# One TensorE signal per slot, and per pair of slots, in a graph network's two gather stages

## What is computed

```python
x = _layernorm(x + L0(x, edge_attr_64, ...))
x = _layernorm(x + L1(x, edge_attr_64, ...))
# L0:
h = concatenate([x[src], edge_attr], axis=1) @ W1 + b1
msg = silu(batchnorm(h) * g1 + be1)
agg = segment_sum(msg, dst) / maximum(count(dst), 1)
out = silu(batchnorm(concatenate([x, agg], axis=1) @ W2 + b2) * g2 + be2)
# L1:
msg = relu(x[src] + edge_attr)
out = relu(((1 + eps) * x + segment_sum(msg, dst)) @ W.T + b)
```

## Time and profile before

| | us |
|---|---|
| runs | 10119.3, 10121.98, 10125.19; median 10121.98 |
| profiled execution, first to last instruction (span) | 10108.7 |
| POOL busy | 5970.4 (59%) |
| PE busy / PEld busy | 4398.6 (44%) / 2780.5 (28%) |
| DVE / ACT busy | 1864.3 (18%) / 1239.0 (12%) |
| gathers of the first stage (line 371), 3125 | 2968.4 busy, first start 29.5, last 4588.5 |
| gathers of the second stage (line 1194), 3125 | 2971.8 busy, first start 5445.6, last 9967.5 |

### The profile page before, as it was taken

One profiled execution on the slowest core, in us unless ns is written; L12 is line 12 of the kernel. 1 busy time (PEld: TensorE's weight loads), 2 busy tenths in 40 slices (PEclk: granted clock), 3 DMA queues, 4 the chain that ended last, 5 costly groups with the idle time before them and its releaser, 6 DMA issues. The chain is left out here.

```text
span 10108.7 us, 90454 instructions
## 1 busy us (share of the span) xinstructions
PE 4398.6 (44%) x25778; PEld 2780.5 (28%) x25778; DVE 1864.3 (18%) x4868; ACT 1239.0 (12%) x2056; POOL 5970.4 (59%) x6272
## 2 busy tenths in 40 slices
PE   3433443434444444347984333333333334333335
PEld 1222222222222222226872222222222222222222
DVE  2111111111111111116763000000000000000002
ACT  0000000000000000004664000000000000000001
POOL 6666666666666666660003666666666666666662
PEclk7666666666666666668996666666666666666666
DMA  3222222222222222224551121121112212111111
GB/s 79 68 67 66 69 67 66 69 67 67 68 67 68 68 67 67 68 67 132 164 151 50 44 47 45 45 45 45 45 45 45 45 45 46 44 45 45 45 45 33
DMA packets 800217, 638.49 MB, mean 63 GB/s; under 512 B 532451, under 2 KB 618703, under 8 KB 799368
## 3 DMA queue, kind: packets, MB, share of 16 engines
q1 hardware_dynamic: 553308, 326.50, 12.0%
q0 software_dynamic: 200416, 208.55, 10.7%
q10 hardware_dynamic: 46400, 102.52, 3.1%
HBM read 528.15 MB, written 108.90 MB: 63 GB/s over the span
## 5 line engine op out<-in xcount | busy, mean ns | idle before, releaser
L1194 POOL DMA_INDIRECT X<-x_scratch,src_idx x3125 | 2971.8, 951 | 1624.3 <-issue 893.6
L371 POOL DMA_INDIRECT Z<-in_x_dram,src_idx x3125 | 2968.4, 950 | 1611.1 <-issue 895.1
L416 PE MATMUL PS<-ZT,W_sb 128*64 128x320 f32 x2500 | 1198.0, 620 | 2716.5 <-ACT ZT L456 2391.7
L1216 PE MATMUL PS<-hot_c,msg_c 128*64 128x48 f32 x6250 | 658.9, 271 | 2765.6 <-issue 1733.5
L1216 PEld LDWEIGHTS PS<-hot_c,msg_c 128*64 128x64 f32 x6250 | 575.0, 184 | 3163.0 <-issue 2048.4
L416 PEld LDWEIGHTS PS<-ZT,W_sb 128*64 128x64 f32 x2500 | 396.7, 185 | 3153.5 <-issue 2160.2
L522 DVE BATCH_NORM_STATS2 stats<-PS 128x320 f32 (+1 forms) x624 | 279.3, 490 | 3670.2 <-remote 3451.3
L456 ACT ACTIVATE ZT<-PS 128x640 f32<-128x640 f32 x625 | 425.2, 702 | 4150.2 <-remote 3395.5
L1252 DVE TENSOR_TENSOR table<-table,PS 64x48 f32 x625 | 130.2, 208 | 4057.3 <-DMA shares_scratch<-counts 3495.7
L1235 ACT ACTIVATE msg_c<-PS 128x320 f32<-128x320 f32 x625 | 260.0, 436 | 4295.3 <-DMA counts_scratch<-table 2919.9
L1205 PE MATMUL PS<-E,ident 128*128 128x320 f32 x1250 | 689.6, 644 | 11.8 <-DMA E<-in_edge_attr_dram 11.8
(11 more groups left out here) (135 smaller groups left out, 2519.8 us busy)
## 6 DMA issues: line engine op xcount, KB each, us to landing
Z<-in_edge_attr_dram SPq DMA_DIRECT2D x625, 160.0 KB
E<-in_edge_attr_dram SPq DMA_DIRECT2D x625, 160.0 KB
h_scratch<-h_ring ACTq DMA_DIRECT2D x312, 320.0 KB
hT<-h_scratch SPq DMA_DIRECT2D x312, 320.0 KB
Z<-in_x_dram,src_idx POOLq DMA_INDIRECT x3125
X<-x_scratch,src_idx POOLq DMA_INDIRECT x3125
x_nodes<-in_x_dram SPq DMA_DIRECT2D x1, 3125.0 KB
x_ring<-in_x_dram SPq DMA_DIRECT2D x25, 125.0 KB
```

Of the source, the lines that this page charges most:

```text
L371: nc.gpsimd.indirect_dma_start(out=Z[:, r, j, 0:D], out_offset=None, in_=x, in_offset=bass.IndirectOffsetOnAxis(ap=src_idx[:, n:n + 1], ax ...
L416: nc.tensor.matmul(PS[ab * D:(ab + 1) * D, bank + c, 0:HC], W1_sb[:, :], ZT[:, s % 2, c * HC:(c + 1) * HC], start=True, stop=True)
L1194: nc.gpsimd.indirect_dma_start(out=X[:, r, j, :], out_offset=None, in_=x1_dram, in_offset=bass.IndirectOffsetOnAxis(ap=src_idx[:, n:n + 1] ...
L1216: last = nc.tensor.matmul(PS[D:P, 2 + s % S, 0:WIN], msg[:, s % S, j, :], hot[:, s % S, j, :], start=(j == 0), stop=(j == TG - 1))
```

## The change

The first gather stage keeps its work, and its signals `rows_done` and `dense_done` become one, `pe_step`, given once for the first transposes and then at the end of every `dense(s)`; as PE's order is `turn_rows(s + 1)`, `dense(s)`, the value s + 2 tells of both. All who waited for either now wait for it.

The second gather stage works in pairs of slots: one edge load, one relu, one one-hot of two slots, and one signal `pe_step` after the pair's segment sums in place of `sum_put` and `summed` per slot. Edge sums take PSUM banks 0-3, segment sums 4-7. POOL waits at even slots only. The diff, cut (waits of SP, the written-out last slot and some DVE lines are left out):

```diff
-            rows_done = sem("rows_done")
+            pe_step = sem("a_pe_step")
...
-            dense_done = sem("dense_done")
...
-                            pool.wait_ge(rows_done, g + 1 - RING)
+                            pool.wait_ge(pe_step, g + 1 - RING)
...
                             last = nc.tensor.transpose(banks(2 * (s % 2), 2, P, EG)[:, j * P:(j + 1) * P],
                                                        Z[:, r, j, :], ident[:, :])
-                        last.then_inc(rows_done, 1)
+                        return last
...
                                                     hot[:, q % 5, ab, j, :], start=(j == 0), stop=(j == TG - 1))
-                        last.then_inc(dense_done, 1)
+                        last.then_inc(pe_step, 1)
...
-                    turn_rows(0, 0)
+                    turn_rows(0, 0).then_inc(pe_step, 1)
...
-                            act.wait_ge(rows_done, at(k, BODY, s + 1))
-                            wait_at(act, dense_done, k, BODY, s - 1)
+                            act.wait_ge(pe_step, at(k, BODY, s + 1))
...
-                        dve.wait_ge(dense_done, at(k, BODY, 2 * q + 2))
+                        dve.wait_ge(pe_step, at(k, BODY, 2 * q + 3))
...
-            E = sb(here, "E", [P, RING, TG, D])
+            E = sb(here, "E", [P, S, 2, TG, D])
...
-            msg = sb(here, "msg_c", [P, S, TG, D])
-            hot = sb(here, "hot_c", [P, S, TG, WIN])
+            msg = sb(here, "msg_c", [P, 2, 2, TG, D])
+            hot = sb(here, "hot_c", [P, 2, 2, TG, WIN])
...
-                        if g >= RING:
-                            pool.wait_ge(sum_put, g + 1 - RING)
+                        if g >= RING and g % 2 == 0:
+                            pool.wait_ge(pe_step, (g - RING) // 2 + 1)
...
-                    def edge_sum(k, s):
-                        r = s % RING
-                        wait_at(pe, msg_ready, k, BODY, s - 1)
...
+                    def edge_sum(k, q, slots):
+                        wait_at(pe, msg_ready, k, 10, q - 1)
+                        pe.wait_ge(e_loaded[q % S], at(k, 32, 16 * (q // S) + 16))
+                        for a in range(slots):
+                            r = (2 * q + a) % RING
+                            to = PS[:, 2 * (q % 2) + a, 0:HC]
+                            nc.tensor.matmul(to, ident[:, :], E[:, q % S, a, :, :].rearrange("p t c -> p (t c)"),
+                                             start=True, stop=False)
+                            pe.wait_ge(gathered[r], at(k, 32 * TG, 16 * TG * (2 * q // RING) + 16 * TG))
+                            last = nc.tensor.matmul(to, ident[:, :], X[:, r, :, :].rearrange("p t c -> p (t c)"),
+                                                    start=False, stop=True)
+                        return last
+
+                    def segment_sum(k, q, slots):
+                        pe.wait_ge(hot_ready, at(k, 10, q + 1))
+                        pe.wait_ge(msg_ready, at(k, 10, q + 1))
+                        wait_at(pe, added, k, BODY, 2 * q - 2)
+                        for a in range(slots):
+                            for j in range(TG):
+                                last = nc.tensor.matmul(PS[D:P, 4 + 2 * (q % 2) + a, 0:WIN], msg[:, q % 2, a, j, :],
+                                                        hot[:, q % 2, a, j, :], start=(j == 0), stop=(j == TG - 1))
+                        last.then_inc(pe_step, 1)
...
+                        for q in range(slots // 2):
+                            edge_sum(k, q + 1, 1 if slots < BODY and q + 1 == slots // 2 else 2)
+                            segment_sum(k, q, 2)
...
+                    def relu(k, q, slots):
+                        act.wait_ge(pe_step, at(k, 10, q + 1))
+                        act.activation(msg[:, q % 2, 0:slots, :, :].rearrange("p a t c -> p a (t c)"),
+                                       PS[:, 2 * (q % 2):2 * (q % 2) + slots, 0:HC], ACT.Relu).then_inc(msg_ready, 1)
...
+                    def one_hot(k, q, slots):
+                        wait_at(dve, pe_step, k, 10, q)
...
+                    def add(k, s, firsts):
+                        dve.wait_ge(pe_step, at(k, 10, s // 2 + 2))
```

More of the change, by code:

```diff
@@ L1211, in segment_sum @@
-                    def segment_sum(k, s):
-                        pe.wait_ge(hot_ready, at(k, BODY, s + 1))
-                        pe.wait_ge(msg_ready, at(k, BODY, s + 1))
-                        wait_at(pe, added, k, BODY, s + 1 - S)
-                        for j in range(TG):
-                            last = nc.tensor.matmul(PS[D:P, 2 + s % S, 0:WIN], msg[:, s % S, j, :], hot[:, s % S, j, :],
-                                                    start=(j == 0), stop=(j == TG - 1))
-                        last.then_inc(summed, 1)
@@ L1220, in body @@
-                    def body(k, slots):
-                        for s in range(slots):
-                            if not (slots < BODY and s == slots - 1):
-                                edge_sum(k, s + 1)
-                            segment_sum(k, s)
-                    edge_sum(0, 0)
+                    def edge_sum(k, q, slots):
[10 more added lines that the diff above has]
+                        return last
@@ L1227, in _ @@
+                    def body(k, slots):
+                        for q in range(slots // 2):
+                            edge_sum(k, q + 1, 1 if slots < BODY and q + 1 == slots // 2 else 2)
+                            segment_sum(k, q, 2)
+                        if slots < BODY:
+                            segment_sum(k, slots // 2, 1)
+                    edge_sum(0, 0, 2).then_inc(pe_step, 1)
                     all_bodies(pe, body)
@@ L1230, in _ @@
                 def _(act):
+                    def relu(k, q, slots):
+                        act.wait_ge(pe_step, at(k, 10, q + 1))
+                        act.activation(msg[:, q % 2, 0:slots, :, :].rearrange("p a t c -> p a (t c)"),
+                                       PS[:, 2 * (q % 2):2 * (q % 2) + slots, 0:HC], ACT.Relu).then_inc(msg_ready, 1)
                     def body(k, slots):
[L1232 to L1236 removed]
+                        for q in range(slots // 2):
+                            relu(k, q, 2)
+                        if slots < BODY:
+                            relu(k, slots // 2, 1)
                     all_bodies(act, body)
@@ L1249, in add @@
-                    def add(k, s, first):
-                        dve.wait_ge(summed, at(k, BODY, s + 1))
+                            hot[:, q % 2, 0:slots, :, :].rearrange("p a t w -> p (a t) w"),
+                            window[:, :].unsqueeze(1).to_broadcast([P, slots * TG, WIN]),
+                            rel5[:, ds(at(k, BODY, 2 * q), slots), :].rearrange("p a t -> p (a t)").unsqueeze(2)
+                            .to_broadcast([P, slots * TG, WIN]), ALU.is_equal).then_inc(hot_ready, 1)
@@ L1255, in body @@
                     def body(k, slots):
-                        for s in range(slots):
-                            if s % S == 0:
-                                load_windows(dve, at(k, 4, s // S))
-                                firsts = windows_of_turn(dve)
-                            if not (slots < BODY and s == slots - 1):
-                                one_hot(k, s + 1)
-                            add(k, s, firsts[s % S])
-                    one_hot(0, 0)
+                        firsts = {}
@@ new lines, in body @@
+                        for q in range(slots // 2):
+                            for t in range(-(-2 * q // S), (2 * q + 1) // S + 1):
+                                firsts[t] = load_pair_windows(dve, at(k, 4, t), t % 2)
+                            one_hot(k, q + 1, 1 if slots < BODY and q + 1 == slots // 2 else 2)
+                            add(k, 2 * q, firsts)
+                            add(k, 2 * q + 1, firsts)
+                        if slots < BODY:
+                            add(k, 2 * (slots // 2), firsts)
@@ L1265, in _ @@
+                    one_hot(0, 0, 2)
                     all_bodies(dve, body)
```

43 lines of the change are left out of this document (14 added, 29 removed).

## The result

The changed kernel takes 10141.49 us (median of 20 runs, 10130.47 to 10149.35) against 10122.22 (20 runs, 10108.18 to 10133.9): ratio **1.0017, 95% interval 1.001 to 1.0023**. The forecast was 10056, faster; the range, 9520 to 10180, holds the measured time, but it is wide enough for either direction, and the direction was wrong. The profiled spans are 10142.4 and 10108.7 us. The 13 us between span and median that I carried over from before are not there after, where the span is 1.8 us under the time of its own execution: most of the 13 us will have been a quick profiled execution. So the spans show 34 us where the medians show 19, and what a stage differs by from the profile of before may be some 12 us too large.

A forecast was written before the change was run, and what follows sets the result against it. The prediction took POOL's gathers, plus its stops while TensorE's finished signals are held, to bound the kernel. Second stage -124, first stage +50, its end +8: -66 us, from 10121.98 to 10056 us, range 9520 to 10180.

The forecast's parts named there:

- the second stage's term: Second gather stage: one signal per pair gives runs of 16 slots, 0.75 us of stop per slot instead of 0.95, -124 us.
- I take their median, 12.: Second stage: TensorE's signal is held 12 us, the median of six held times from 6.9 to 28.1; hence 15.3 us per pair.
- the low end of my term: Second stage, signal held 28 us: runs of only six slots, 0.92 us of stop per slot, -20 us.
- The stop line: POOL's stops: length follows a straight line, 1.9 us + 0.13 per gather in the run before.
- All a change beside the gathers can win: 1232 us: Both gather stages: POOL's stops of 640 and 592 us are all that can be won, 12% of the span.
- counted as 0: Second stage: VectorE's one-hot for two slots at once runs beside POOL and costs nothing.
- +50 taken: First stage: one signal under way at a time, runs half of three slots (+100 us), half of four (0); +50 us.
- 8 were taken: End of the first stage: TensorE works off ten slots with one more ACT round each, about +8 us.
- Rival 3: Both stages: signals are not what is short, runs and stops stay as they are; 10122 us within 20, chance 0.12.
- one passage in 12.55 us: Second stage, argument against rival 3: two slots need only one signal passage in 12.55 us; rows show 8.3 and 6.9.
- Rival 1: Second stage: signals held under 9.2 us, so POOL never stops; -534 us, 9588 us, chance 0.23.
- Rival 2: First stage, ACT's copy: one signal at a time costs more than the second wins; two-slot runs, 10336 us; chance 0.17.

The follow-up runs named there:

- e7_dve_sums: Against the kernel before: in the second stage VectorE adds gathered and edge rows, POOL waits for VectorE, TensorE signals once per five slots; ratio 1.0043, second stage 4562 us.
- e15: The changed kernel plus a useless 1000-column POOL fill after each first-stage slot's gathers; ratio 0.9966 to the kernel before, first stage 4509 us.

## Why the prediction was wrong, step by step

**The step that failed is the second stage's term: "I take their median, 12."** It failed with what followed from it, 15.3 us per pair, runs of sixteen slots and -124 us; the profiles show six slots and -3 us. I treated the held time as a time per signal. The rows had a better reading: of the first run's signals, 28.1 us stood behind a segment sum (ten loads and ten matmuls) and 11.1 behind an edge sum (four and four): 1.40 and 1.39 us per TensorE instruction, the very pace that `e7_dve_sums` shows (1.39 while POOL gathers). A pair's signal stands behind 56 instructions, at that pace an estimated 77 us, not 12; no run of gathers is long enough to show the whole of it, but of the 103 signals sent from 10 to 25 us after POOL's restart 98 were held until its stop. So runs have six slots, not sixteen. That was the low end of my term (n = 6: -20 us).

**The stop line held and hid the bound.** 1.9 us + 0.13 per gather gives 5.8 us after 30 gathers; measured 5.81. But it has a constant of 1.9 us per stop, and I read a gain from longer runs into it. 50 gathers took 11.1 us (`e7`), 175 took 29.7: 0.17 to 0.22 us per gather with no constant worth the name (20: 4.45, 0.22). "All a change beside the gathers can win: 1232 us" has no run behind it: over seventeen versions the second stage took 1.42 to 1.49 us per gather.

**The one-hot, "counted as 0", cost 37 us.** Beside the 0.66 us one-hot of a pair, gathers take 1.34 and 1.43 us (6280.91 and 6323.09) instead of 0.94; after the change nearly every run starts with one. The 210 gathers that start during a one-hot take together 54 us more than they would at 944 ns each; before, 180 such gathers took 18 us more. The difference is the whole cost. The second stage's account: stops -54 us, the short gaps that took the place of dropped stops +14, gathers +37: -3 us. The Trainium skill (SBUF — State Buffer, "Who interferes with whom") says that a VectorE instruction with two SBUF inputs contends with a GpSimd one that reads SBUF. The trace agrees: `L1251` has two, and lengthens the gathers that start during it (1203 ns in the mean; those already under way keep 945); the table adds, with one input in PSUM, do not (946 ns beside them).

**The first stage came near what was argued.** Runs of three and four slots, +50 taken, +35 measured, from one signal under way at a time. (In parts: stops +35, short gaps -18, gathers +18, of which 14 are gathers that start during a one-hot. The second stage starts 5 us later still; 8 were taken.) A stretch there (before: the earlier trace rows):

```profile
1998.05 0.70 ACT L454 ACTIVATE ZT<-PS 128x640 f32<-128x640 f32 x1 [3.91 <-PE PS L422]
...
2000.03 0.77 PE L404 MATMUL PS<-ident,Z 128*128 128x128 f32 x5
...
2012.52 0.70 ACT L454 ACTIVATE ZT<-PS 128x640 f32<-128x640 f32 x1 [13.76 <-remote]
...
2013.29 0.94 POOL L370 DMA_INDIRECT Z<-in_x_dram,src_idx  x1 [3.67 <-remote]
```

The signal behind the dense matmuls, which end as the transposes of 2000.03 begin, is held some 12.5 us, and nothing else is under way. What I had not seen are the runs of five: POOL often stops twice (60 times 2.2 us after 15 and then 2.8 after 5, medians) for the 4.45 us that it stood once after 20. As I read it, one signal comes out at a stop where up to four did. In `e15` the loss is gone with the stops; that this is all of its cause is argued from there.

**The rivals.** Rival 3 had the right bound (stops go with the gathers before them). Its time, 10122 within 20, came out by 19 us, but with luck: it had runs and stops unchanged, and they changed in both stages, with parts that nearly cancel. It lost most of its weight to my sentence that one passage in 12.55 us would do. Rival 1 is refuted by the changed kernel itself, in which the fourth signal of a run is held 30 us, not under 9.2, and by `e7`, which needs no passage for some 90 us and still stops. Rival 2 had the direction and the place, ACT's copy in the first stage, which cost more than the second stage won. Its condition, runs of two slots, was not met (5 runs of 229), and its form with runs of three, 10169, took too much for both: +100 in the first stage, -61 in the second.

So the result splits into -0.38% for the pairs, +0.27% and +0.28% for the merged signals, each to some 0.15%. What the runs leave open is what the gathers owe, if not their transfers, and why TensorE alone waits for it; no run tried to name it. Each time on record comes with a profiled span and clock, so whether the profiler's recording has a part in it is open too.

## What to carry to other kernels

Before you price a wait, see whether the held time goes with the number of signals, of instructions, or with what another engine has done since it last stood still: two held times behind work of different size would have told it here. Stops that keep the same sum when you cut them differently are a debt, not a latency; the cheap test is to put useless work on the engine that stops, and if the time stays, the stops are not what to remove. Here it paid to merge work and not signals: in the first stage several signals under way passed a slow stretch better than one, and in the second one signal for everything put more one-hots beside gathers.

## What the runs showed of the chip that I had not expected

- In a long run of indirect gathers TensorE gets through one load or matmul in 1.39 us, against 160 in 7 us when POOL has stood long enough, though the gathers' packets have landed 1.3 us after the last of them (`e7_dve_sums`); ACT and VectorE keep their durations.
- A gather of half the rows is 52 ns shorter (median 892 against 944), and the stage no shorter.
- 594 us of useless POOL work made a kernel 0.4% faster: stops, short gaps and gathers fell by 630 us.
